# A vision-transformer tower: VectorE work moved to ScalarE, and the weights' preparation split between the first groups

## The reference

```python
h = concat(cls_tok, patches @ W.T + b)                 # 17 tokens an image
# 1  attention, 12 heads of 64: per row the diagonal is masked, the 12 largest scores
#    are kept, the heads' mean score is added, then softmax, values, projection
# 2  two "bit-linear" layers (192 -> 1024, gate * up, 512 -> 192):
scale = 127 / max(max|x|, 1e-5); xq = clip(round(x * scale), -128, 127) / scale
wq = clip(round(w / mean|w|), -1, 1) * mean|w|         # ternary weights
# 3  linear attention, 12 heads of 16, cumulative over the tokens, with a gate
#    tanh(amp * cos(phase)) from a small network
# 4  relu layer 192 -> 128 -> 192 and a second matrix Wo, then a layer norm
```

## Time and profile before

| what | value |
|---|---|
| runs | 650.09, 635.8, 645.94 us; median 645.94 |
| profiled execution | 637.83 us, its span 636.0 us |
| mean granted TensorE clock | 0.97 of full |
| busy, share of the span | PE 91%, DVE 78%, ACT 41%, POOL 52% |
| chain that ended last | PE 52%, DVE 34%, issue 7%, ACT 3%, POOL 2% |
| transfers | 14.66 MB, nearly all in the first 36 us |

### The profile page before, as it was taken

The page is one execution under the profiler, slowest core; times in us unless marked ns, Lnnn a source line. Parts: engine busy times, 40 slices in busy tenths (PEclk is TensorE's granted clock), DMA queues, the critical chain, the costliest instruction groups (busy, mean ns, idle before and its releaser), DMA issues.

```text
span 636.0 us, 15302 instructions
## 1 busy us (share of the span) xinstructions
PE 576.3 (91%) x5133; PEld 460.8 (72%) x5139; DVE 496.9 (78%) x2078; ACT 260.0 (41%) x659; POOL 331.2 (52%) x826
## 2 busy tenths in 40 slices
PE   4778789999999999999999999999999999878885
PEld 4457477877878787878778787878787787755551
DVE  0684558888888989898888889898988889887632
ACT  2134154453535353454536353544535352523310
POOL 2110015564737474655647474756557374745753
PEclk9899779999999999999999999999999999989977
DMA  9810010000000000000000000000000000000000
GB/s 234 193 48 1 6 41 1 23 1 25 27 7 24 7 23 8 24 6 22 13 20 22 6 22 6 22 6 22 6 6 6 6 1 7 3 6 1 8 7 7
DMA packets 11060, 14.66 MB, mean 23 GB/s; under 512 B 2160, under 2 KB 8657, under 8 KB 11017
## 3 DMA queue, kind: packets, MB, share of 16 engines
q1 hardware_dynamic: 8712, 12.44, 7.3%
q10 hardware_dynamic: 2304, 1.67, 0.9%
HBM read 12.44 MB, written 1.67 MB: 22 GB/s over the span
## 4 chain that ended last, share of the span: by engine, by line
PE 52%; DVE 34%; issue 7%; ACT 3%; POOL 2%; DMA 1%; DVEq 0%; SPq 0%; POOLq 0%; ACTq 0%
PE bank_att L1355 6%; PE bank_lin L1448 6%; PE bank_embed L1277 5%; DVE kept L750 5%; DVE scores L730 4%; PE bank_att L1129 4%; PE bank_att L1344 4%; PE bank_embed L1282 3%; DVE stats L701 3%; DVE top L742 2%; PE bank_lin L1465 2%; PE bank_embed L1240 2%; PE bank_lin L1129 2%; DVE norms L855 2%; PE bank_att L1312 2%
## 5 line engine op out<-in xcount | busy, mean ns | idle before, releaser
L496 POOL TENSOR_TENSOR spread<-moments,gain_eps 119x1 f32<-119x1 f32 x57 | 12.4, 217 | 159.1 <-DVE moments L703 159.1
L1277 PE MATMUL bank_embed<-norm0T,w_qkv 128*128 128x119 f32 (+1 forms) x456 | 58.6, 279 | 3.1 <-ACT v L1015 2.1
L497 POOL TENSOR_TENSOR rstd<-spread,minus_half 119x1 f32<-119x1 f32 (+1 forms) x95 | 56.6, 595 | 7.5
L1277 PEld LDWEIGHTS bank_embed<-norm0T,w_qkv 128*128 128x128 f32 x456 | 55.2, 195 | 5.5 <-ACT v L1015 4.5
L775 DVE TENSOR_TENSOR weightsT<-bank_lin,consts 119x476 f32<-119x476 f32 (+1 forms) x57 | 35.6, 628 | 20.7 <-PE bank_lin L1448 20.7
L497 POOL TENSOR_TENSOR rstd_h<-spread_h,minus_half 119x12 f32<-119x12 f32 x19 | 43.3, 2277 | 1.5
L1240 PE MATMUL bank_embed<-w_tok,patchT 128*119 128x192 f32 (+1 forms) x228 | 42.8, 340 | 0.9 <-ACT patchT L999 0.9
L1448 PE MATMUL bank_lin<-feat_qk,feat_k 32*119 32x119 f32 (+1 forms) x456 | 40.6, 272 | 0.4 <-ACT tanh_par L1088 0.4
L1355 PE MATMUL bank_att<-w_o,att0T 128*119 128x192 f32 (+1 forms) x228 | 40.2, 326 | 0.0
L730 DVE TENSOR_REDUCE scores<-bank_att 119x51 f32<-119x357 f32 (+1 forms) x76 | 38.0, 504 | 2.3 <-PE bank_att L1312 0.3
L988 ACT COPY att1T<-bank_lin 96x238 f32<-96x238 f32 (+1 forms) x19 | 6.6, 346 | 80.8 <-PE bank_lin L1129 80.8
(11 more groups left out here) (244 smaller groups left out, 1495.2 us busy)
## 6 DMA issues: line engine op xcount, KB each, us to landing
strips<-x SPq DMA_DIRECT2D x18, 336.0 KB
out<-result ACTq DMA_DIRECT2D x18, 89.2 KB
w_qkv<-L_attn_w_qkv SPq DMA_DIRECT2D x2, 576.0 KB, 7.2
w_in_raw<-L_ffn_w_in SPq DMA_DIRECT2D x1, 768.0 KB, 12.0
w_tok_raw<-L_tok_W SPq DMA_DIRECT2D x1, 576.0 KB
w_qkv_rest<-L_attn_w_qkv SPq DMA_DIRECT2D x2, 288.0 KB, 9.0
w_o<-L_attn_w_out SPq DMA_DIRECT2D x1, 576.0 KB
w_qkv_raw<-L_attn_Wqkv SPq DMA_DIRECT2D x1, 432.0 KB
```

What stands on the lines that cost most here:

```text
L497: pool.tensor_tensor(rstd_out, spread, minus_half[0:ROWS, 0:spread.shape[1]], ALU.pow) \
L1277: pe.matmul(parts((E0, E1)[s], 3)[:, j, 0:r], w_qkv0[:, tile * 128:(tile + 1) * 128], norm0T[:, s, 0:r], start=j == 0, stop=False, skip_gr ...
```

## The change

Five things.

1. The last third of the probabilities is spread by ScalarE: `a_wide` issues seven activations, one an image, each a copy of 4 heads x 17 columns (68) scaled by one column of the mask. `v_wide(2)` leaves VectorE's list.
2. ScalarE also does the first half of both roundings: big_in and big_out are activations with a scale operand and the constant as bias, followed by the old subtraction, on a new counter `run_a_quant`. VectorE ends with the scale (quant_in, quant_out). `v_u_in` and `p_scaled` wait on that counter before they overwrite what ScalarE reads.
3. The turning of the weights is cut into `setup_turns` (w1, wo, half of w_in), `turn_w_in((2, 3))` and `turn_w_out`, each a step of the list in turn 1 only (`for_group`), with ScalarE's copies likewise. The bias products (`setup_biases`) and w2 by wo (`setup_w2o`) become steps in turn 2. The last product, b2o, goes behind turn 3.
4. All four lists are reordered.
5. The zero products get other places and numbers, with some in the first turns (banks A0, L1).

```diff
+        def for_group(pieces):
+            def step(g, p):
+                if isinstance(g, int) and g in pieces:
+                    pieces[g]()
+            return step
...
             def p_scaled(g, p):
                 pool.wait_ge(S["product"], g + 1)
+                after(pool, RUN["a_quant"], 2 * g)
...
-                (4, p_gate), (0, p_strips), (3, p_scaled), (3, p_rms), (5, p_h3_beta), (5, p_rstd4), (4, p_centred_sq),
-                (4, p_rstd_h), (3, p_rstd2), (0, p_rstd0), (4, p_rstd3), (2, p_rstd1), (3, p_feat_k), (0, p_h0),
+                (5, p_rstd3), (0, p_strips), (4, p_feat_k), (4, p_gate), (3, p_scaled), (3, p_rms), (5, p_h3_beta),
+                (5, p_rstd4), (4, p_centred_sq), (4, p_rstd_h), (3, p_rstd2), (0, p_rstd0), (0, p_h0), (2, p_rstd1),
...
             def v_u_in(g, p):
...
                 dve.wait_ge(S["moments1"], g + 1)
+                after(dve, RUN["a_quant"], 2 * g - 1)
...
-                in_chain(g, dve.tensor_scalar(quant_in[:, :], ainv_in[:, :], rstd1[:, 0:1], 127.0, ALU.mult, ALU.mult))
-                dve.tensor_scalar(big_in[:, :], u_in[:, :], quant_in[:, 0:1], ROUND, ALU.mult, ALU.add) \
-                    .then_inc(S["big_in"], 1)
+                dve.tensor_scalar(quant_in[:, :], ainv_in[:, :], rstd1[:, 0:1], 127.0, ALU.mult, ALU.mult).then_inc(S["quant_in"], 1)
...
-                (3, v_big_in), (2, v_wide(1)), (2, v_wide(2)), (5, v_stats4), (4, v_causal[0]), (3, v_gated), (4, v_causal[1]),
-                (4, v_causal[2]), (4, v_v1), (3, v_big_out), (4, v_ratio), (4, v_sq_sum), (2, v_h1), (2, v_u_in),
-                (1, v_pack(0, A0)), (3, v_h2), (3, v_stats2), (1, v_pack(1, A1)), (5, v_result), (4, v_att1), (0, v_h0),
-                (0, v_stats0), (3, v_norms2), (1, v_pack(2, A0)), (0, v_norm0), (1, v_pack(3, A1)), (1, v_top), (1, v_drop),
-                (4, v_h3), (4, v_stats3), (1, v_mix), (4, v_norm3), (3, v_feat), (1, v_probs), (3, v_hidT), (1, v_wide(0)),
+                (3, v_big_in), (4, v_causal[0]), (2, v_wide(1)), (5, v_stats4), (4, v_causal[1]), (4, v_causal[2]),
+                (3, v_gated), (4, v_v1), (3, v_big_out), (4, v_ratio), (5, v_result), (4, v_sq_sum), (2, v_h1), (2, v_u_in),
+                (3, v_h2), (3, v_stats2), (1, v_pack(0, A0)), (1, v_pack(1, A1)), (4, v_att1), (3, v_norms2), (0, v_h0),
+                (0, v_stats0), (1, v_pack(3, A1)), (1, v_pack(2, A0)), (0, v_norm0), (1, v_top), (1, v_drop), (4, v_h3),
+                (4, v_stats3), (1, v_mix), (4, v_norm3), (3, v_feat), (3, v_hidT), (1, v_probs), (1, v_wide(0)),
...
+            def a_wide(g, p):
+                act.wait_ge(S["probs"], g + 1)
+                after(act, S["turned2"], g)
+                for b in range(PER):
+                    last = act.activation(wide[:, 8:12, b], probs[:, 8:12, :], ACT.Copy,
+                                          scale=block_mask[:, b * TOKENS:b * TOKENS + 1])
+                last.then_inc(S["widened2"], 1)
...
             def a_int_in(g, p):
-                act.wait_ge(S["big_in"], g + 1)
+                act.wait_ge(S["quant_in"], g + 1)
+                act.activation(big_in[:, :], u_in[:, :], ACT.Copy, scale=quant_in[:, 0:1], bias=ROUND).then_inc(RUN["a_quant"], 1)
+                act.wait_ge(RUN["a_quant"], 2 * g + 1)
                 act.activation(int_in[:, :], big_in[:, :], ACT.Copy, bias=-ROUND).then_inc(S["int_in"], 1)
...
-                (5, a_hid1), (3, a_int_in), (3, a_in_T), (2, a_probsT[0]), (1, a_qk(0)), (3, a_tanh_gate), (2, a_probsT[2]),
...
+                (3, a_int_in), (2, a_probsT[0]), (3, a_in_T), (1, a_qk(0)), (3, a_tanh_gate), (4, a_interference),
+                (2, a_probsT[1]), (2, a_probsT[2]), (3, a_square), (1, a_qk(1)), (4, a_num_T), (2, a_att[0]), (2, a_att[1]),
+                (3, a_int_out), (3, a_out_T), (0, a_patchT(1, E1, S["patches1"], S["patchT1"])),
...
+                (0, a_v(0)), (0, a_v(1)), (0, for_group({1: copy_w_out})), (3, a_tanh_hid), (1, a_exp), (5, a_store), (4, a_norm3_T), (3, a_tanh_par),
+                (1, a_wide), (4, a_hid1),
...
-            setup = [setup_sums_of_weights, setup_turns, setup_biases]
+            setup = [setup_sums_of_weights, lambda: None, lambda: late_setup(pe), setup_b2o]
...
-                (5, zero_products(E0, {15: 2})), (5, t_out4), (3, t_int_in), (2, t_probs(0)), (2, t_probs(1)), (3, t_gate),
...
-                (4, zero_products(E0, {18: 6})), (4, t_norm3), (3, t_params), (4, t_hid1), (3, zero_products(E0, {17: 2})),
-                (3, t_lin((0, 1), S["a_done01"])),
+                (5, t_hid1), (4, zero_products(E0, {16: 1})), (4, t_lin((0, 1), S["a_done01"])),
+                (5, zero_products(E0, {17: 3})), (5, t_out4), (0, zero_products(L1, {2: 3})),
+                (2, zero_products(A0, {2: 2}, True)), (2, t_probs(0)), (3, t_int_in), (0, zero_products(L1, {3: 2})),
+                (4, t_lin((2,), S["a_done2"])), (3, t_gate), (2, zero_products(E0, {18: 1})), (2, t_probs(1)), (2, t_probs(2)),
+                (1, t_qk(1)), (4, zero_products(E0, {16: 6, 17: 6})), (4, t_num), (2, t_att0(0)), (2, t_att0(1)),
+                (0, zero_products(L1, {2: 4})), (4, t_num_turn), (2, t_proj0), (3, zero_products(E0, {18: 4})), (3, t_int_out),
+                (0, zero_products(A0, {0: 2})), (0, zero_products(L1, {3: 4})),
+                (0, t_patches(1, E1, S["k_copied1"], S["patches1"])), (0, t_patches(0, E0, S["k_copied0"], S["patches0"])),
+                (3, zero_products(E0, {17: 5})), (3, t_down), (1, t_dots(0)), (0, t_embed),
+                (0, for_group({1: setup_turns, 2: setup_biases})), (1, t_dots(1)),
+                (4, zero_products(E0, {16: 10, 17: 10, 18: 10})), (4, t_att1), (3, zero_products(E0, {18: 4})), (3, t_norms2),
+                (4, t_proj1), (0, t_norm0), (0, zero_products(A0, {0: 2})), (0, for_group({1: lambda: turn_w_in((2, 3))})),
+                (3, t_qk1), (0, t_v), (0, zero_products(A0, {0: 4})), (0, for_group({1: turn_w_out, 2: setup_w2o})),
+                (3, t_hid), (4, zero_products(E0, {18: 10})), (4, t_norm3), (0, t_qk(0)), (3, t_params),
```

More of the change, by code:

```diff
@@ L316, in build @@
             proj0 h1
-            moments1 rstd1 unit_in half_c2 big_in int_in in_turned in_copied gate_done up_done tanh_gate
-            product scaled square_sum mean_square rms_inv big_out int_out out_turned out_copied down_done h2
+            moments1 rstd1 unit_in half_c2 quant_in int_in in_turned in_copied gate_done up_done tanh_gate
+            product scaled square_sum mean_square rms_inv quant_out int_out out_turned out_copied down_done h2
             stats2 moments2 rstd2 norms2 norms_turned norms_copied qk1 hid relu_qk feat_q feat_k_all feat_k
@@ L326, in build @@
         S = {n: sem("s_" + n) for n in step_names}
-        RUN = {n: sem("run_" + n) for n in "v_att v_in v_out v_lin v_last p_ffn p_lin p_gate p_head p_last".split()}
+        RUN = {n: sem("run_" + n) for n in "v_att v_in v_out v_lin v_last p_ffn p_lin p_gate p_head p_last a_quant".split()}
         strips_in = [sem("strips_in0"), sem("strips_in1")]
@@ L835, in v_big_out @@
                 out_chain(g, dve.reciprocal(ainv_out[:, :], amax_out[:, :]))
-                out_chain(g, dve.tensor_scalar(quant_out[:, :], ainv_out[:, :], row_gain[:, 0:1], 127.0, ALU.mult, ALU.mult))
-                dve.tensor_scalar(big_out[:, :], scaled[:, :], quant_out[:, 0:1], ROUND, ALU.mult, ALU.add) \
-                    .then_inc(S["big_out"], 1)
+                dve.tensor_scalar(quant_out[:, :], ainv_out[:, :], row_gain[:, 0:1], 127.0, ALU.mult, ALU.mult) \
+                    .then_inc(S["quant_out"], 1)
             def v_h2(g, p):
@@ L1061, in a_int_out @@
             def a_int_out(g, p):
-                act.wait_ge(S["big_out"], g + 1)
+                act.wait_ge(S["quant_out"], g + 1)
+                act.activation(big_out[:, :], scaled[:, :], ACT.Copy, scale=quant_out[:, 0:1], bias=ROUND).then_inc(RUN["a_quant"], 1)
+                act.wait_ge(RUN["a_quant"], 2 * g + 2)
                 act.activation(int_out[:, :], big_out[:, :], ACT.Copy, bias=-ROUND).then_inc(S["int_out"], 1)
@@ L1143, in step @@
                             pe.wait_ge(S["k_copied0"], GROUPS)
+                        if bank_tile is L1 and g > 2:
+                            pe.wait_ge(setup_row, 2)
+                        if scores_read:
+                            pe.wait_ge(S["packed2"], g + 1)
+                            pe.wait_ge(S["packed3"], g + 1)
                         multiply_zeros(bank_tile, counts[g])
@@ L1182, in setup_turns, with turn_w_in @@
                 pe.wait_ge(setup_ternary, 1)
-                for n in range(4):
+                turn_w_in((0, 1))
+            def turn_w_in(quarters):
+                for n in quarters:
                     if n >= 2:
@@ L1361, in t_int_in @@
                 pe.wait_ge(S["int_in"], g + 1)
+                if isinstance(g, int) and g == 1:
+                    pe.wait_ge(setup_row, 4)
```

40 lines of the change are left out of this document (19 added, 21 removed).

## The result

The changed kernel takes 662.34 us (median of 4 runs, 660.0 to 667.74) against 644.86 for the kernel before in the runs beside it: ratio 1.0371, interval 1.0304 to 1.0438. It is slower. I had said 636, with 622 to 650 as range and 0.10 for slower. The profiled execution took 667.74 us with a span of 665.8, which is 29.8 more than the 636.0 of before. The two profiles lie further apart than the kernels: the one of before is of a short execution (637.83 for a median of 644.86), the one of after of its longest, and the medians are only 17.5 apart. Medians and ranges here are over all executions, while a ratio leaves out those over 1.5% above the fastest of their kernel (among them two of e1 at 676, without which its median is 650.3, and one of e2 at 673).

A forecast was written before the change was run, and what follows sets the result against it. TensorE bounds the middle turns, with work for 28.12 of 29.00 us. Gains of 1.4 (fourteen turns), 3.2 (start) and 1.0 (end), 5.6 together, off 641.9 give 636; own range 632 to 641, 8 in 10 622 to 650.

The forecast's parts named there:

- 0.10 for slower: Chance given to a time over 655 us: far half of the rival without overlap of the seven pieces, plus scatter.
- the last sentence on the turn: Middle turns: GpSimd's scaled goes behind the gate instead of the strips, about 1 us earlier, nobody waits for it last; 0.
- TensorE's wait for norm3: Middle turns: TensorE turns norm3 before the q product and waits 0.38 us for VectorE, bounds 0 to 0.6.
- out4's wait: Middle turns: TensorE's out4 waits 0.40 us (0.24 to 1.20) for hid1T, behind ScalarE's seven wide pieces of 1.57.
- my two rows: Seven ScalarE pieces, from a PSUM copy's row 1.41 us, from an SBUF-reading row 1.72; middle taken, 1.57.
- The clock: Start: full clock on the q product at 68.82 would save 1.4 us, but VectorE sets that end; counted 0.
- the two waits: Middle turns: new TensorE waits for norm3 (0.38) and hid1T (0.40), making a turn 28.89 us, a gain of 0.10.
- The end: Last turns: big_out's 0.49 us leaves VectorE's queue twice, a gain of 1.0 us (0 to 3); zero products 0.
- The start: Fourth turn starts at 77.1, 2.0 us earlier, k product at about 81.9 instead of 85.93; net gain 3.2 (0 to 6).
- the two small transfers: Start: transfers on SyncE's queue before the fourth turn, landing at most 2.4 us after release, bounded by the 79.06.
- The slower one: Rival, chance 0.12: the seven ScalarE pieces don't overlap and take 2.37 us, turn 29.69, time 647.5.
- The one in which ScalarE's queue eats the gain: Rival, chance 0.15: the seven pieces last 1.72 to 1.8 us, turn 29.1, time 639.

The follow-up runs named there:

- e1: The changed kernel with GpSimd's copy of strips to patches moved back behind the gate step; 652.37 us, 650.3 by the executions the ratio keeps.
- e2: The kernel before with only GpSimd's new order, without the wait on run_a_quant; 657.75 us.
- e4: The changed kernel with the copy of strips behind the gate step and the third wide product back on VectorE; 640.43 us, median of ten runs.
- e3: The changed kernel with the third wide product back on VectorE, ScalarE's seven pieces gone; 651.21 us.
- e9: The changed kernel with the copy of strips at its new place but waiting until norm3 is done; 650.97 us.
- e7: The changed kernel with the copy of strips split into two copies of half the size; 659.17 us.
- e5: The changed kernel with four zero products ahead of the turn of norm3, acting in the unrolled turns only; 665.92 us.
- e8: e4 with both roundings also back on VectorE; 635.15 us, ratio to the kernel before 0.9924.
- e6: e4 with six zero products in the turn in which the last group is in its first stage; 635.02 us, ten runs.
- e12: e8 with the six zero products of e6; 636.35 us.
- e11: e8 with the weight preparation in one piece again and the first turns' zeros as in the kernel before; 647.68 us median, one of four runs 635.0.

## Why the prediction was wrong

**The step that failed** is the last sentence on the turn: GpSimd's new order, "about 1 us earlier, nobody waits for it last", costed at 0. It looked only for who waits for GpSimd's results. What it missed is what the moved copy runs beside. Undone alone it gives 0.85 us a turn back (e1, and e4 against e3), done alone to the kernel before it takes 0.5 (e2), and with the overlap alone taken away (e9) the place costs next to nothing (29.1 for e1's 29.0): over the fourteen turns with a long norm3, 0.85 x 14 is 11.9 of the 29.8 us. The trace of before had shown it. At the fourth turn unit_in, two columns wide, takes 0.98 us right behind the start of the same copy at 79.23, and 0.228 in the median (the second row: minimum, median, maximum in ns):

```profile
79.31 0.98 DVE L812 TENSOR_SCALAR unit_in<-unit_gain,amax_in 119x2 f32<-119x2 f32 x1
...
L812 DVE TENSOR_SCALAR unit_in<-unit_gain,amax_in x19: 228/228/978, 79.3 to 590.7; 119x2 f32<-119x2 f32 x19
```

And it had shown it in turn after turn, on an instruction that I did not look at: probs, with both inputs in SBUF, takes 0.84 in fifteen turns, beside feat_k on GpSimd, and 0.37 in the first two turns, in which no feat_k runs beside it. It ends 0.23 behind the second feat_k. In before hidT, which TensorE waits for, stands right behind it, and the new order puts hidT ahead. (VectorE, GpSimd, then minimum, median, maximum; that feat_k is the cause is argued from these rows and not tested.)

```profile
336.94 0.84 DVE L766 TENSOR_TENSOR probs<-expd,exp_inv 119x204 f32<-119x204 f32 x1
```
```profile
336.43 1.12 POOL L547 TENSOR_TENSOR feat_k<-feat_qk,consts 96x238 f32<-96x238 f32 x2
```
```profile
L766 DVE TENSOR_TENSOR probs<-expd,exp_inv x19: 370/839/841, 44.8 to 567.5; 119x204 f32<-119x204 f32 x19
```

The Trainium skill has the rule, in "SBUF — State Buffer", under Who interferes with whom: VectorE and GpSimd share a pair of ports that is given whole to whichever instruction comes first, and tensor_scalar between SBUF tensors can be in the mode that needs it, while an instruction with at most one SBUF input outside that mode does not contend. The traces agree: norm3 1.22 beside the copy, 0.79 beside half of it (e7), the two weightsT with one input in PSUM 1.20 as ever (e4), and the copy 1.22 when feat_qk, with two SBUF inputs, came first (e9). They show the lengths and not the ports, and which of norm3 and the copy was issued first they don't show.

**TensorE's wait for norm3** was right in its mechanism and nearly in its size. From the end of the second scores (335.19 + 0.89) to 343.15 TensorE takes 7.07, as counted. Take the 0.85 off the 1.17 and 0.32 is left, which e4 shows as 0.32; the forecast was 0.38.

**out4's wait** was right as a mechanism and too small: 0.63 for 0.40, because the seven pieces take 1.79 and not the middle value 1.57. The estimate worked out from the figures of the Trainium skill ("ScalarE: Activation LUTs", What ACT_TABLE_LOAD costs), 1.79 and 0.62, agrees with the trace; of my two rows the one that shares the memory (0.339 a piece, measured 0.342) was the nearer, and the mean with the one out of PSUM was the error. It cost 0.23 in each of fifteen turns, 3.4 us.

**The clock** I counted at 0 everywhere. In the middle it fell in four turns, 4 x 1.6 = 6.4 us. In the profiled executions these falls go with the two waits: with either of them shortened there are two, none or none (e1, e3, e9), with both none (e4). So the two waits cost about 13 us directly, and the 6.4 may be theirs too. That is not shown: only one execution of each kernel was profiled, e2 has four long turns with a single wait of another kind, and the kernel before, without these waits, loses as much clock in its own longer executions. Those beside e5 to e8 run from 635.57 us at a mean clock of 0.973 to 653.9 at 0.943; as an estimate from these that is 34 us at the lower level in one and 74 in the other, against 69 in the profile of after and a median of 62 over its four executions. The clock is thus much of why the profiles are 29.8 apart, and the 13 us of the waits are the larger part of the 17.5 between the medians.

**The end.** I had -1.0; it was +10.8, of which 7.6 in the 16th turn (34.7 for 27.1), which ran at half clock from about 562 to 580. This isn't from the two waits, e4 has it too. The changed places of the zero products don't start it either: neither kernel has a product of zeros between 110 us and this point. The two profiles with TensorE's old order (before, e2) are without it, but so are e6, e8 and e12 with the new one: it comes and goes with edits that shift the last groups by fractions of a microsecond (e8 and e4 differ by the roundings alone). The kernel before itself runs between 635.6 and 654, three executions of over 1000 us at full clock left aside. What exactly decides it stays open, and no run put TensorE's old order of the end back alone; as far as the times tell, e4 was without it in two of ten runs, e6 with its zeros in all ten, and e8 without them likewise.

**The start.** I had -3.2. amax_in came at 78.16, 0.9 earlier instead of 2.0: VectorE's additions ended at 76.75, later than counted, and it then waited for the two small transfers that I had only bounded. The k product came at 84.91 instead of 81.9; three pairs of products ahead of it ran at 1.06 instead of 0.6, at the low clock, which I had put at 0 as well. By the first parameter product 0.6 was left. The runs show no more for the split than the 1.2 of e11. From the forecast of -5.6 to the 29.8 of the profiles it is 35.4: norm3 11.9 less 0.8 (the rest of its wait was forecast too long), out4 3.4, the clock in the middle 6.4, the end 11.8, the start 2.6, together 35.3.

**The rivals.** The slower one, seven pieces without overlap, did not happen: 7 x 0.342 would be 2.39, they took 1.79. The one in which ScalarE's queue eats the gain (pieces of 1.72 to 1.8 together) had that part right. None had a cost on VectorE from GpSimd.

## What to carry to other kernels

When a step on GpSimd is moved, look at what VectorE runs in its new stretch, and not only at who waits for its result: a long GpSimd copy started by the same release as a short critical VectorE instruction added most of its length to it here (0.84 of 1.03 us). The cure is a place beside VectorE's work on PSUM, or a wait that lets the short one in first. In a trace, look for instructions much longer than the minimum of their group: the page books the time held off as busy time. And compare turns one by one before a mean over them is trusted, since some ran 1.6 us longer at a lower clock, and ask where in the spread of its kernel a profiled execution lies.

Three of the kernels here are a little faster than both given ones, by 0.5 to 0.8% with intervals clear of 1: e8 (0.9924, 0.9887 to 0.9961), which keeps of the change the order of VectorE, ScalarE and TensorE and the split, e6 and e12. In the profiles their lead is a turn of 28.6 or 28.7 for 29.0; their starts and ends are no shorter than those of before (e8: first parameter product at 108.15 for 106.76, from the 16th on 95.8 for 95.0). What else sets them ahead of before by the medians is that no execution of theirs is as long as its longer ones.

## What the runs showed that I had not expected

- A VectorE instruction of 0.38 us took 1.22 beside one GpSimd copy of 1.03, and 0.79 beside one of 0.61; the profile shows this as busy time, with no wait in the row. In before probs does the same in fifteen turns.
- Who is second pays: the copy itself grew to 1.22 when a VectorE product with two SBUF inputs was under way.
- Seven column-scaled activations of 68 columns, SBUF to SBUF, take 1.79 us together and 0.342 each.
- TensorE, busy in all of 535 to 537, fell to the lower clock at about 538 and stayed there for 17 us of work without a gap (e4), while the same stream with the same products of 34 columns, a few tenths of a microsecond apart, kept full clock until about 555 (e8).
